# 16-wide heads' contexts turned in 32x32 blocks on VectorE, first loads on two queues, half of pass 2's masks on VectorE

## The chip, the cores and the metric

The kernel runs on one core of a Trainium2 chip. The metric is the device time of one execution in microseconds (us), the median of several runs. The engines are TensorE (PE), VectorE (DVE), ScalarE (ACT), GpSimd (POOL) and SyncE (SP, which here only issues DMAs). Each works through its own instructions in a fixed order and waits on semaphores.

## The reference, cut to what matters

Input is x of 32 batch elements, 256 rows of 256 float32, and a context of 120 rows of 256 for each. Four transformer layers are applied one after the other; all have 16 heads, in the first three of width 16, in the last of width 64.

```python
# layer 0: pre-norm; self-attention (causal), cross-attention, GELU feed-forward
x = x + attention(ln(x), ln(x), causal) @ W_aproj + b
x = x + attention(ln(x), context) @ Wcproj + b
x = x + gelu(ln(x) @ W_fc + b) @ W_mproj + b
# layer 1: post-norm; self-attention with one mask for all, cross-attention, ReLU feed-forward
x = ln(x + attention(x, x, mask_SxS) @ o_w + b)
x = ln(x + attention(x, context) @ co_w + b)
x = ln(x + relu(x @ lin1_w + b) @ lin2_w + b)
# layer 2: cross-attention with a mask for each element; layer 3: cross-attention, heads of width 64
x = ln(x + attention(x, context, mask_BxSxS2) @ wo)
x = ln(x + attention64(x, context) @ w_fc)
```

`attention` projects q, k and v, takes softmax(q k^T / 4) per head and multiplies by v.

## The kernel before

**Passes.** The kernel goes over the 32 elements three times: pass 1 (`l0`) is layer 0, pass 2 (`l1`) layer 1, pass 3 (`l2`) layers 2 and 3. x goes through device memory between them. Each pass is a list of steps per engine (`LISTS`), each step with a time in units of one element; `Step` adds the element's number and a start of the pass (`START`, `SPREAD`), and `run` sorts them. So several elements are in flight, and each engine's order is the sorted list. A step is named kind.key.number; key is `own` for self-attention (and layer 2's), `other` for the cross-attention of passes 1 and 2.

**One attention of 16-wide heads** (two per element in passes 1 and 2, one in pass 3; 160 in all). `project_q` and `project_k` are computed on PE and copied by ACT into `ot_raw` as float32 (named `other_words` in part for the cross-attention). DVE and POOL split them into three bfloat16 parts, and SP writes the parts to memory (`spill`) and loads them back stacked (`stack`). `scores_max` gets each row's maximum (PE, then DVE). Its negative is split too (`negate`), turned by PE (`negate_t`), copied by DVE to `nm_t` and moved by SP into the stack (`nm_rows`). `scores_exp` computes each head's scores minus the maximum, keys along partitions, and ACT takes the exponential into `probs`.

**Masks.** In pass 1 POOL zeroes what is not causal (L629). In pass 2 PE adds the mask to every head's scores by a matmul of `mask_less` with the identity. In pass 3 DVE takes the minimum of each pair of heads' probabilities and a mask of 0 and 2 (`mask_probs`, L1038).

**The context.** `probs_v` (PE, four steps of four heads) gives, for each head, 32 partitions by 256 queries: 16 rows of the unnormalised context, and a row with the sum of the probabilities. Two steps share a bank of 128x512 float32. Then:

- ACT copies the two banks to `ot_raw` (L672).
- `heads_q`, twice: PE turns it by 8 transposes in all, L1358, so that queries lie along partitions.
- `heads_rec` and `heads_q` on DVE: the reciprocal of the sums (L1069) and the product into `ctx_q` (L1076).
- `heads_t`: PE turns `ctx_q` back by 4 transposes (L1207), ACT copies it to `ctx_t`.
- `project_out`: PE multiplies `ctx_t` by the output weights.

**The first loads.** ACT issues all of them, 35 DMAs, before its first computation (L649 to L667): the vectors in columns and three weights that pass 1 wants first, the other weights and vectors of pass 1, the masks, and last the vectors of passes 2 and 3. PE's banks are eight; `take` waits until the last user of a bank has been read.

Lines of `L1140` are all matmuls through the helper `mm`.

## Time and profile before

| | |
|---|---|
| median of 3 runs | 4811.43 us (4810.87 to 4811.61) |
| profiled execution | 4819.19 us |
| its span, first to last instruction | 4817.4 us |
| PE busy | 4665.7 us, 97% |
| DVE busy | 3353.2 us, 70% |
| ACT busy | 2622.3 us, 54% |
| POOL busy | 1369.9 us, 28% |
| instructions | 101571 |

Busy time is the union of an engine's instructions. Matmuls overlap, so the time that one takes away from PE is the distance from its start to the next start, not its length. Pass 1 lies between 0 and about 1500 us, pass 2 up to about 3200, pass 3 after that.

### The profile page before, as it was taken

Reading aid. Unit: us, or ns where it says so; the run is one execution under the profiler, and the core shown is the slowest. Engines: PE = TensorE matmul, PEld = TensorE weight load, DVE = VectorE, ACT = ScalarE, POOL = GpSimd, SP = SyncE. Lnnn points to the kernel's source line nnn. Section 1 sums busy time; section 2 is a strip of 40 time slices with the busy share of each in tenths; the row PEclk is TensorE's granted clock in tenths of the full one; section 3 lists DMA queues with packets and bytes.
Section 4 is the critical chain, followed back from the end, with each engine's and each line's share of the span. In section 5 each row is a group of like instructions: output and inputs, shape, how many; then the busy total and the mean of one; then the engine's idle time right before and its main releaser. Section 6 shows DMA issues by size and latency. Waiting matters only on the chain. (4 is left out here: it accounts for less than half of the span.)

```text
span 4817.4 us, 101571 instructions
## 1 busy us (share of the span) xinstructions
PE 4665.7 (97%) x36479; PEld 3761.6 (78%) x36544; DVE 3353.2 (70%) x10821; ACT 2622.3 (54%) x6913; POOL 1369.9 (28%) x1813
## 2 busy tenths in 40 slices
PE   4999999999999999999999999989999999999998
PEld 3788888888887778878788787867777777777776
DVE  3677777777777766766667666656676766767674
ACT  1556656565665445454444544535565656565655
POOL 2343333333333123233332333322121212121212
PEclk8999999999999999999999999999999999999999
DMA  4444444444444344444444444432222222222211
GB/s 142 130 126 141 124 143 126 138 130 129 144 121 143 119 128 131 123 121 132 131 131 118 118 131 123 124 92 65 71 60 68 62 65 66 62 67 61 70 58 32
DMA packets 393288, 513.56 MB, mean 107 GB/s; under 512 B 109136, under 2 KB 360784, under 8 KB 371280
## 3 DMA queue, kind: packets, MB, share of 16 engines
q1 hardware_dynamic: 379008, 490.25, 34.6%
q10 hardware_dynamic: 13776, 16.81, 1.2%
q8 instruction: 290, 4.75, 0.4%
q14 instruction: 214, 1.75, 0.1%
HBM read 266.30 MB, written 236.72 MB: 104 GB/s over the span
## 5 line engine op out<-in xcount | busy, mean ns | idle before, releaser
L756 ACT ACTIVATE probs_own<-bank 128x384 f32<-128x384 f32 (+2 forms) x1280 | 607.3, 570 | 682.0 <-remote 361.2
L1140 PE MATMUL bank<-ht,w_ff 128*128 128x256 f32 x2048 | 493.3, 384 | 2.3 <-ACT ht L675 2.2
L1140 PE MATMUL bank<-w_ff,ffh 128*128 128x256 f32 x2048 | 489.3, 382 | 2.0 <-DVE ffh L1113 1.5
L574 POOL TENSOR_SCALAR veps<-meanvar 128x2 f32<-128x2 f32 x256 | 77.2, 302 | 1408.7 <-DVE meanvar L915 1408.2
L1022 DVE TENSOR_REDUCE nmf_other<-bank 128x4 f32<-128x480 f32 x512 | 311.1, 650 | 158.0 <-PE bank L1140 157.6
L1140 PEld LDWEIGHTS bank<-ht,w_ff 128*128 128x128 f32 x2048 | 372.6, 191 | 58.8 <-issue 12.8
L1140 PEld LDWEIGHTS bank<-w_ff,ffh 128*128 128x128 f32 x2048 | 374.6, 190 | 49.3 <-DVE ffh L1113 2.5
L1140 PE MATMUL bank<-qstack_own,kstack_own 99*128 99x256 bf16 (+2 forms) x2560 | 397.2, 266 | 15.4 <-DMA qstack_own<-nm_t_own 8.8
L1018 DVE CUSTOM_DVE_ANT_0 bank<-bank,mask_rows 128x256 f32<-128x256 f32 x1024 | 393.3, 463 | 13.0 <-PE bank L1140 13.0
L841 ACT ACTIVATE probs_other<-bank,negmax 128x120 f32<-128x120 f32 x1024 | 355.5, 375 | 43.9 <-DVE negmax L1120 43.9
L1140 PE MATMUL bank<-kstack_own,qstack_own 96*128 96x256 bf16 (+2 forms) x3072 | 353.7, 245 | 18.3 <-DMA qstack_own<-q_parts 16.1
L643 POOL TENSOR_TENSOR other_parts<-other_words,other_parts 128x240 bf16<-128x240 f32 (+1 forms) x128 | 114.5, 904 | 846.8 <-issue 418.1
L1140 PE MATMUL bank<-ht,w_own 128*128 128x256 f32 x1280 | 314.7, 389 | 24.1 <-ACT ht L675 24.1
L1140 PEld LDWEIGHTS bank<-qstack_own,kstack_own 99*128 99x128 bf16 (+1 forms) x2560 | 230.5, 106 | 118.2 <-DMA qstack_own<-nm_t_own 27.5
L1140 PEld LDWEIGHTS bank<-kstack_own,qstack_own 96*128 96x128 bf16 x3072 | 252.4, 98 | 89.0 <-issue 14.1
L756 ACT ACTIVATE probs_other<-bank 120x512 f32<-120x512 f32 x512 | 283.1, 611 | 57.3 <-PE bank L1140 54.2
L1140 PE MATMUL bank<-probs_own,v_aug_own 128*32 128x256 f32 (+2 forms) x5120 | 292.3, 364 | 6.9 <-POOL probs_own L629 1.6
L1018 DVE DVE_READ_ACCUMULATOR2_ANT nmf_own<- 128x1 f32 x2048 | 289.3, 141 | 0.0
L1140 PEld LDWEIGHTS bank<-ht,w_own 128*128 128x128 f32 x1280 | 232.9, 192 | 70.0 <-issue 42.9
L643 POOL TENSOR_TENSOR k_parts_own<-ot_raw_own,k_parts_own 128x512 bf16<-128x512 f32 (+1 forms) x96 | 96.0, 1000 | 652.7 <-DVE k_parts_own L975 652.7
L1120 DVE TENSOR_REDUCE negmax<-bank 128x4 f32<-128x480 f32 x256 | 155.8, 650 | 179.8 <-PE bank L1140 178.8
L1018 DVE CUSTOM_DVE_ANT_0 bank<-bank,m_rows 128x120 f32<-128x120 f32 x1024 | 247.7, 322 | 44.1 <-PE bank L1140 44.1
(172 smaller groups left out, 10899.1 us busy)
## 6 DMA issues: line engine op xcount, KB each, us to landing
qstack_own<-q_parts SPq DMA_DIRECT2D x96, 768.0 KB, 7.1
kstack_own<-k_parts SPq DMA_DIRECT2D x64, 768.0 KB, 5.5
qstack_other<-q_parts SPq DMA_DIRECT2D x64, 768.0 KB, 5.8
q_parts<-q_parts_own SPq DMA_DIRECT2D x96, 384.0 KB, 2.6
k_parts<-k_parts_own SPq DMA_DIRECT2D x64, 384.0 KB, 2.6
q_parts<-q_parts_own SPq DMA_DIRECT2D x96, 256.0 KB, 2.2
q_parts<-other_parts SPq DMA_DIRECT2D x64, 384.0 KB, 2.6
other_words<-k_parts SPq DMA_DIRECT2D x64, 360.0 KB, 3.4
```

Source lines behind the costliest of these rows:

```text
L574: nc.gpsimd.tensor_scalar(veps[key][:, :], meanvar[key][:, :, 1], r["norms"][key]["eps"], None, ALU.add).then_inc(veps_ready.sem, 1)
L643: nc.gpsimd.tensor_tensor(f3[2], x32, f3[1], ALU.subtract).then_inc(lo_ready.sem, 1)
L756: nc.scalar.activation(probs[key][0:rows, j % a.slots, 0:n], bank_of(u)[0:rows, 0:n], ACT.Exp, scale=a.scale).then_inc(a_done.sem, 1)
L841: ins = nc.scalar.activation(probs3[:, j % 4, n, :], bank[:, n * S2:(n + 1) * S2], ACT.Exp, scale=-1.0, bias=negmax3[:, j, n:n + 1], accum ...
L1018: ins = v.tensor_tensor_reduce(scores, scores, add, -1.0, LIMIT if a.masked == "each" else 3.0e38, ALU.add, ALU.min, nmf[key][:, t, at:at ...
L1022: ins = v.tensor_reduce(nmf[key][:, t, first:first + FT * len(heads) - FT + 1:FT], bank[:, 0:len(heads) * nk].rearrange("p (h k) -> p h k" ...
L1120: v.tensor_reduce(negmax3[:, j, :], bank_of(u)[:, 0:HG * S2].rearrange("p (h k) -> p h k", k=S2), AX_X, ALU.min).then_inc(negmax3_ready.se ...
L1140: return nc.tensor.matmul(out, lhsT, rhs, start=first, stop=True, skip_group_check=True)
```

## The change

**Turning the contexts.** `heads_q` and `heads_t` are gone, and with them 12 PE transposes and 3 ACT copies per attention. DVE's transpose works on blocks of 32x32, each turned in its place. DVE now reads each `probs_v` bank and writes it to `ot_raw` with all blocks turned (128x512, twice), takes the reciprocal of the 128x32 sums (`heads_rec`), multiplies (`heads_mul`, two operations of 256 elements) and turns the 128x512 `ctx_q` back in blocks into `ctx_t` (`heads_back`). The rows of the output weights are permuted on the host to fit the order in which the contexts then lie.

```diff
+            elif kind == "probs_v":
...
+                v.transpose(ot_raw[key][:, 2 * j:2 * j + 2, :].rearrange("p g x -> p (g x)"), bank_of(u, ("probs_v", key, 2 * j))[:, :]).then_inc(
+                    d_done.sem, 1)
...
             elif kind == "heads_rec":
-                if w.new(d_full, ("heads_q", key, j)):
-                    dve.wait_ge(d_full.sem, w.value(d_full, ("heads_q", key, j)))
-                by_head = bank_of(u, ("heads_q", key, j))[:, :].rearrange("p (h x) -> p h x", h=H)
-                v.reciprocal(rec[key][:, j, :], by_head[:, :, D]).then_inc(recip_ready.sem, 1)
-            elif kind == "heads_q":
-                if w.new(recip_ready, ("heads_rec", key, j)):
-                    dve.wait_ge(recip_ready.sem, w.value(recip_ready, ("heads_rec", key, j)))
-                if w.new(a_full, ("heads_t", key, 0), 1):
-                    dve.wait_ge(a_full.sem, w.value(a_full, ("heads_t", key, 0), 1))
-                by_head = bank_of(u)[:, :].rearrange("p (h x) -> p h x", h=H)
-                v.tensor_tensor(ctx_q[key][:, j, :].rearrange("p (h d) -> p h d", d=D), by_head[:, :, 0:D],
-                                rec[key][:, j, :, None].broadcast_to((P, H, D)), ALU.mult).then_inc(d_done.sem, 1)
+                for tag in w.latest_first(d_done, [("probs_v", key, i) for i in range(2)]):
+                    if w.new(d_done, tag):
+                        dve.wait_ge(d_done.sem, w.value(d_done, tag))
+                v.reciprocal(rec[key][:, :], ot_raw[key][:, :, :].rearrange("p g (b x) -> p (g b) x", x=32)[:, :, D]).then_inc(recip_ready.sem, 1)
+            elif kind == "heads_mul":
+                if w.new(recip_ready, ("heads_rec", key, 0)):
+                    dve.wait_ge(recip_ready.sem, w.value(recip_ready, ("heads_rec", key, 0)))
+
+                src = ot_raw[key][:, :, :].rearrange("p (a i) (b x) -> p a i b x", a=2, x=32)
+                dst = ctx_q[key][:, :, :].rearrange("p t c -> p (t c)").rearrange("p (a b i d) -> p a i b d", a=2, i=2, d=D)
+                by = rec[key][:, :].rearrange("p (a i b) -> p a i b", a=2, i=2)
+                for n in range(2):
+                    ins = v.tensor_tensor(dst[:, n], src[:, n, :, :, 0:D], by[:, n, :, :, None].broadcast_to((P, 2, T // 32, D)), ALU.mult)
+                ins.then_inc(divided.sem, 1)
+            elif kind == "heads_back":
+                if w.new(divided, ("heads_mul", key, 0)):
+                    dve.wait_ge(divided.sem, w.value(divided, ("heads_mul", key, 0)))
+                if w.new(d_full, ("project_out", key, 0), 1):
+                    dve.wait_ge(d_full.sem, w.value(d_full, ("project_out", key, 0), 1))
+                v.transpose(ctx_t[key][:, :, :].rearrange("p f t -> p (f t)"), ctx_q[key][:, :, :].rearrange("p t c -> p (t c)")).then_inc(
+                    context_ready.sem, 1)
```

PE's `project_out` waits for `heads_back`, and ACT's `project_q` and `project_k` of the next element wait for `heads_mul`:

```diff
-                tag = latest(w, d_full, "heads_q", key, QT, 1)
-                if w.new(d_full, tag, 1):
-                    act_e.wait_ge(d_full.sem, w.value(d_full, tag, 1))
+                if w.new(divided, ("heads_mul", key, 0), 1):
+                    act_e.wait_ge(divided.sem, w.value(divided, ("heads_mul", key, 0), 1))
...
             elif kind == "project_out":
                 arrive(key + "_o")
-                if w.new(a_done, ("heads_t", key, 0)):
-                    pe.wait_ge(a_done.sem, w.value(a_done, ("heads_t", key, 0)))
+                if w.new(context_ready, ("heads_back", key, 0)):
+                    pe.wait_ge(context_ready.sem, w.value(context_ready, ("heads_back", key, 0)))
```

**Masks.** In pass 2 the heads with an even number get `mask_probs` on DVE instead of the mask matmul; the odd ones keep it. The setup has four more operations: three with the first five, and one after a PE step `masks`, which stands at 1.25 in pass 1's first element.

```diff
-              "dve", "pe")
+              "dve", "half")
...
+            masks.l1.1/1.25
...
+            ff_mid.ff.2/3.8731 ff_out.ff.0/4.1553 masks.l1.0/1.2 masks.l1.1/1.3
```

**First loads.** ACT keeps four of them. Eighteen go to SP, right after the first load of x; the thirteen for passes 2 and 3 go to SP too, one by one at 4.00 to 7.00 elements.

```diff
+            if kind == "loads":
+
+                if key == "first":
+                    for dst, src in passes[0]["v_loads"]:
+                        sp.dma_start(dst, src).then_inc(v_loaded, 16)
+                    for n in ("other_qkv", "own_o"):
+                        for dst, src in passes[0]["weights"][n][1]:
+                            sp.dma_start(dst, src).then_inc(arrived[n], 16)
+                    for dst, src in passes[0]["late_loads"]:
+                        sp.dma_start(dst, src).then_inc(late_loaded, 16)
+                    for n in ("other_o", "ff1", "ff2"):
+                        for dst, src in passes[0]["weights"][n][1]:
+                            sp.dma_start(dst, src).then_inc(arrived[n], 16)
+                    for dst, src in mask_loads:
+                        sp.dma_start(dst, src).then_inc(masks_loaded, 16)
+                else:
+                    dst, src = rest_loads[j]
+                    sp.dma_start(dst, src).then_inc(rest_loaded, 16)
...
     @block.scalar
     def _(act_e):
         w = Where()
-        for sem, loads in (first_loaded, passes[0]["first_loads"]), (v_loaded, passes[0]["v_loads"]):
-            for dst, src in loads:
-                act_e.dma_start(dst, src).then_inc(sem, 16)
-            if sem is first_loaded:
-                for dst, src in passes[0]["weights"]["own_qkv"][1]:
-                    act_e.dma_start(dst, src).then_inc(arrived["own_qkv"], 16)
-        for n in ("other_qkv", "own_o"):
-            for dst, src in passes[0]["weights"][n][1]:
-                act_e.dma_start(dst, src).then_inc(arrived[n], 16)
-        for dst, src in passes[0]["late_loads"]:
-            act_e.dma_start(dst, src).then_inc(late_loaded, 16)
-        for n in ("other_o", "ff1", "ff2"):
-            for dst, src in passes[0]["weights"][n][1]:
-                act_e.dma_start(dst, src).then_inc(arrived[n], 16)
-        for dst, src in mask_loads:
-            act_e.dma_start(dst, src).then_inc(masks_loaded, 16)
-        for one in passes:
-            for dst, src in one["rest_loads"]:
-                act_e.dma_start(dst, src).then_inc(rest_loaded, 16)
+        for dst, src in passes[0]["first_loads"]:
+            act_e.dma_start(dst, src).then_inc(first_loaded, 16)
+        for dst, src in passes[0]["weights"]["own_qkv"][1]:
+            act_e.dma_start(dst, src).then_inc(arrived["own_qkv"], 16)
         act_e.wait_ge(first_loaded, 16 * len(passes[0]["first_loads"]))
```

**Orders.** All lists, `START` and `SPREAD` have other numbers, so every engine's order differs. The places that the prediction speaks of follow.

PE in the middle of pass 2, before. The last `probs_v` of the own attention stands first, then come weights of the next projection, the 8 turns of L1358, small transposes, and the 4 turns of `ctx_q_own` (L1207). `project_out` (`w_own,ctx_t_own`) stands six rows after the end of this piece:

```order
L1140 MATMUL bank<-probs_own,v_aug_own 32x256 x16
L1140 MATMUL bank<-ht,w_own 128x256 x4
L1358 MATMUL bank<-ident,ot_raw_own 128x128 x8
L1188 MATMUL bank<-ident,c_in 128x120 x2
L1297 MATMUL bank<-identb,nm_parts_other 96x128 x2
L1207 MATMUL bank<-ident,xh 128x128 x4
L1140 MATMUL bank<-ht,w_own 128x256 x4
L1140 MATMUL bank<-ht,w_ff 128x256 x4
L1140 MATMUL bank<-qstack_other,other_words 120x256 x10
L1207 MATMUL bank<-ident,ctx_q_own 128x128 x4
```

The same place after. The turns are gone, and `project_out` is the fifth row:

```order
L1148 MATMUL bank<-probs_own,v_aug_own 32x256 x16
L1148 MATMUL bank<-ht,w_own 128x256 x4
L1300 MATMUL bank<-identb,nm_parts_other 96x128 x2
L1148 MATMUL bank<-ht,w_own 128x256 x4
L1148 MATMUL bank<-w_own,ctx_t_own 128x256 x4
L1148 MATMUL bank<-qstack_other,other_words 120x256 x10
```

`project_out` has moved close behind the last `probs_v`.

DVE at this place of pass 2, before (names in brackets are the semaphores that it waits for):

```order
L1064 COPY nm_t_other<-bank 48x256 [waits nm_rows_other,d_full]
L1069 RECIPROCAL rec_own<-bank 128x16
L965 CAST k_parts_own<-ot_raw_own 128x512 [waits a_done,spilled_k_own]
L969 TENSOR_TENSOR ot_raw_own<-ot_raw_own,k_parts_own 128x512 [waits hi_ready]
L975 CAST k_parts_own<-ot_raw_own 128x512 [waits rest_ready,spilled_k_own]
L1069 RECIPROCAL rec_own<-bank 128x16
L1076 TENSOR_TENSOR ctx_q_own<-bank,rec_own 128x256 [waits recip_ready]
L965 CAST q_parts_own<-ot_raw_own 128x512 [waits a_done,spilled_q_own]
L1076 TENSOR_TENSOR ctx_q_own<-bank,rec_own 128x256
```

And after: masks (`mask_cols`), the two block transposes from the banks, the reciprocal, the product, and the transpose back, with steps of other attentions between them:

```order
L1024 TENSOR_TENSOR probs_own<-probs_own,mask_cols 128x512 [waits a_done] x4
L1039 TENSOR_TENSOR nmf_other<-nmf_other,nm_parts_other 128x32 [waits negate_step]
L1041 CAST nm_parts_other<-nmf_other 128x2x16 [waits negate_step]
L1062 STREAM_TRANSPOSE ot_raw_own<-bank 128x512 [waits lo_ready,a_full] x2
L1068 RECIPROCAL rec_own<-ot_raw_own 128x32 [waits d_done]
L1043 TENSOR_TENSOR nm_parts_other<-nmf_other,nm_parts_other 128x2x16 [waits negate_step]
L1077 TENSOR_TENSOR ctx_q_own<-ot_raw_own,rec_own 128x2x8x16 [waits recip_ready]
L1077 TENSOR_TENSOR ctx_q_own<-ot_raw_own,rec_own 128x2x8x16
L1050 COPY nm_t_other<-bank 48x256 [waits nm_rows_other,d_full]
L1084 STREAM_TRANSPOSE ctx_t_own<-ctx_q_own 128x512 [waits divided]
```

The whole turn is now on DVE, behind four of the eight masks.

DVE's first element after, from the negation to the first copy of `nm_t_own`; before, the five setup operations that existed stood behind that copy:

```order
L1039 TENSOR_TENSOR nmf_own<-nmf_own,nm_parts_own 128x32 [waits negate_step]
L1041 CAST nm_parts_own<-nmf_own 128x2x16 [waits negate_step]
L1043 TENSOR_TENSOR nm_parts_own<-nmf_own,nm_parts_own 128x2x16 [waits negate_step]
L1622 TENSOR_SCALAR b_root<-columns_l 128x8 [waits masks_loaded,first_loaded]
L1623 TENSOR_SCALAR mask_rows<-ffh 128x512 [waits setup_v]
L1624 TENSOR_TENSOR vectors_l<-vectors_l,ffh 128x256 [waits setup_v]
L1625 TENSOR_TENSOR vectors_l<-vectors_l,ffh 128x256 [waits setup_v]
L1628 TENSOR_SCALAR mask_less<-ffh 128x512 [waits setup_v]
L1632 TENSOR_REDUCE none_left<-mask_rows 128x2 [waits setup_v]
L1633 TENSOR_SCALAR ffh<-none_left 128x256 [waits setup_v]
L1634 TENSOR_SCALAR mask_cols<-ffh 128x512 [waits setup_v]
L1050 COPY nm_t_own<-bank 48x256 [waits setup_v,d_full]
```

Eight setup operations now stand ahead of `nm_t_own`.

## Rows read from the trace of the kernel before

**Rows 1.** Page, part 1: busy us of each engine, share of the span, instructions

```profile
PE 4665.7 (97%) x36479; PEld 3761.6 (78%) x36544; DVE 3353.2 (70%) x10821; ACT 2622.3 (54%) x6913; POOL 1369.9 (28%) x1813
```

**Rows 2.** Windows: length; busy PE, PEld, DVE, ACT, POOL; clock; DMA share, GB/s

```profile
200.00:1400.00 1200.00, 1193.36 (x9892) 999.81 (x9891) 922.75 (x2103) 724.39 (x1665) 442.28 (x748) 1.00 0.45 132
1800.00:3000.00 1200.00, 1197.39 (x9221) 964.16 (x9265) 829.25 (x3008) 576.07 (x1234) 367.76 (x400) 1.00 0.42 125
3400.00:4600.00 1200.00, 1186.99 (x9185) 934.83 (x9187) 844.14 (x3256) 734.30 (x2482) 239.46 (x250) 1.00 0.22 64
```

**Rows 3.** Once-per-element steps: timeline and tiles x_in, m_in (ns, first and last start)

```profile
64.69 0.41 SPq L475 DMA_DIRECT2D x_in<-in_x  x1
...
L475 SPq DMA_DIRECT2D x_in<-in_x x32: 393/404/449, 0.8 to 1469.5; - x32
...
L609 POOL TENSOR_TENSOR xb<-x_in,vectors_l x32: 1264/1272/1276, 1544.7 to 3137.8; 128x512 f32<-128x512 f32 x32
...
L485 SPq DMA_DIRECT2D m_in<-in_mask_BxSxS_bk x32: 389/400/1455, 3201.3 to 4706.7; - x32
```

**Rows 4.** Timeline of PE, pass 1: start us, length us, instruction, how many

```profile
1015.82 1.99 PE L1140 MATMUL bank<-ht,w_own 128*128 128x256 f32 x8
1017.65 1.04 PE L1358 MATMUL bank<-ident,ot_raw_own 128*128 128x128 f32 x8
1018.52 1.89 PE L1140 MATMUL bank<-ht,w_own 128*128 128x256 f32 x8
1020.25 0.38 PE L1140 MATMUL bank<-qstack_other,other_words 99*120 99x256 bf16 x2
1020.47 0.60 PE L1207 MATMUL bank<-ident,ctx_q_own 128*128 128x128 f32 x4
1020.91 0.38 PE L1140 MATMUL bank<-qstack_other,other_words 99*120 99x256 bf16 x2
```

**Rows 5.** Timeline of PE, pass 2, own scores with the mask

```profile
2499.93 0.38 PE L1140 MATMUL bank<-qstack_own,kstack_own 99*128 99x256 bf16 x2
2500.15 0.38 PE L1140 MATMUL bank<-mask_less,identb 128*128 128x512 bf16 x1
2500.37 0.38 PE L1140 MATMUL bank<-qstack_own,kstack_own 99*128 99x256 bf16 x2
```

**Rows 6.** Groups by line and shape of DVE: count, busy us, mean ns

```profile
L1038 DVE TENSOR_TENSOR probs_own<-probs_own,m_cols 120x512 f32<-120x512 f32 x256 | 157.3, 685 | 12.1 <-ACT probs_own L756 10.5
...
L1076 DVE TENSOR_TENSOR ctx_q_own<-bank,rec_own 128x256 f32<-128x256 f32 x192 | 73.2, 407 | 1.3
...
L1076 DVE TENSOR_TENSOR ctx_q_other<-bank,rec_other 128x256 f32<-128x256 f32 x128 | 49.2, 405 | 0.0
L1069 DVE RECIPROCAL rec_own<-bank 128x16 f32<-128x16 f32 x192 | 48.7, 254 | 132.8 <-PE bank L1358 132.8
...
L1069 DVE RECIPROCAL rec_other<-bank 128x16 f32<-128x16 f32 x128 | 28.3, 242 | 21.5 <-PE bank L1358 21.4
```

**Rows 7.** Timeline of DVE, eleven reductions of a bank back to back

```profile
1038.32 6.67 DVE L1022 TENSOR_REDUCE nmf_own<-bank 128x2 f32<-128x512 f32 x11
```

**Rows 8.** Timeline of the first 40 us, all engines

```profile
2.85 0.49 ACTq L651 DMA_DIRECT2D vectors<-in_L_xattn_b_attn  x1
...
7.17 1.09 PE L1207 MATMUL bank<-ident,xh 128*128 128x128 f32 x4 [7.17 <-DVE xh L927]
...
15.95 0.49 ACTq L664 DMA_DIRECT2D ffh<-in_mask_by_key  x1
...
29.92 1.28 ACT L675 ACT_TABLE_LOAD   x1 [29.92 <-issue]
31.21 1.02 ACT L675 ACTIVATE ht<-bank,columns_l 128x256 f32<-128x256 f32 x2
...
37.56 2.85 SPq L499 DMA_DIRECT2D k_parts<-k_parts_own  x3
```

**Rows 9.** DMA issues: KB of each, median us from issue to landing

```profile
ffh<-in_mask_by_key ACTq DMA_DIRECT2D x1, 256.0 KB, 9.3
```

More of the change, by code:

```diff
@@ L141 @@
[L141 to L144 removed]
+            turn.0.0/0.3024 project_q.own.0/0.5346 project_k.own.0/0.5738 project_v.own.0/0.6704 scores_max.own.1/0.9469
@@ new lines @@
+            scores_exp.own.3/1.3551 scores_exp.own.10/1.3644 scores_exp.own.4/1.3690 scores_exp.own.9/1.3737
+            scores_exp.own.8/1.3829 scores_exp.own.6/1.3876 scores_exp.own.7/1.3922 probs_v.own.0/1.4049
+            scores_exp.own.11/1.4253 probs_v.own.1/1.4365 scores_exp.own.12/1.4568 scores_exp.own.14/1.4615
+            scores_exp.own.13/1.4662 scores_exp.own.15/1.4754 context.c.0/1.4846 probs_v.own.2/1.4911 probs_v.own.3/1.5143
+            project_out.own.0/1.6104 project_k.other.0/1.7256 norm.1.0/1.7869 project_q.other.0/1.8368 project_v.other.0/2.1688
@@ L145 @@
+            probs_v.other.1/2.8256 project_out.other.0/3.2565 norm.2.0/3.7117 ff_in.ff.3/3.7502 ff_in.ff.2/3.8735
+            ff_in.ff.0/3.9101 ff_in.ff.1/3.9702 ff_out.ff.0/4.0208 ff_out.ff.1/4.0808 ff_out.ff.2/4.1275 ff_out.ff.3/4.1871
         """,
         "ACT": """
-            turn.0.0/0.2824 project_k.own.0/0.5466 project_q.own.0/0.5962 scores_exp.own.1/1.2539 scores_exp.own.5/1.2634
-            scores_exp.own.0/1.2729 scores_exp.own.6/1.2919 scores_exp.own.7/1.3014 scores_exp.own.2/1.3109
@@ L411, in run @@
     recip_ready = counts("recip_ready", "DVE", ("heads_rec",))
+    divided = counts("divided", "DVE", ("heads_mul",))
+    context_ready = counts("context_ready", "DVE", ("heads_back",))
     poly_ready = counts("poly_ready", "DVE", ("ff_in",))
@@ L436, in run @@
     arrived = {n: sem(f"arrived_{n}") for n in dict.fromkeys(n for one in passes for n in one["weights"])}
-    n_rest = 16 * sum(len(one["rest_loads"]) for one in passes)
+    rest_loads = [x for one in passes for x in one["rest_loads"]]
+    n_rest = 16 * len(rest_loads)
+    assert len(rest_loads) == sum(u.tag[0] == "loads" for u in plan["SP"]) - 1
     block = ctx.enter_context(nc.Block())
@@ L858, in _ @@
                 if first and j == r["first_of"]["probs_v3"]:
-                    reuse(act_e, w, u, d_full, [("heads_q", "other", i) for i in range(QT)], u.element - 1)
+                    reuse(act_e, w, u, divided, [("heads_mul", "other", 0)], u.element - 1)
                 if w.new(a_full, u.tag):
```

355 lines of the change are left out of this document (163 added, 192 removed), and 6 rows, old and new, of the table SPREAD.

## The prediction

> **What bounds the kernel now.** I read the busy shares first [rows 1]. TensorE (PE) is busy 4665.7 of 4817.4 us; VectorE (DVE) follows at 3353.2. A whole-span share averages three passes, so I cut a window from the steady part of each [rows 2]. PE is busy 1193.4, 1197.4 and 1187.0 of 1200 us, at a granted clock of 1.00, that is its 2.4 GHz level. Of PE's 151.7 idle us only 22 lie in these 3600 us; the other 129 lie in the start, the two changes of pass and the end. So inside a pass the kernel goes at PE's pace, and work taken from PE comes off the time as long as no other engine needs the whole of it. The engine to watch is DVE: 922.8, 829.3 and 844.1 of 1200 us, or 76.9%, 69.1% and 70.3%.
>
> These shares need a time per batch element. An operation that runs once per element gives it [rows 3]: (1469.5 - 64.7)/30 = 46.8 us in pass 1, (3137.8 - 1544.7)/31 = 51.4 in pass 2, (4706.7 - 3201.3)/31 = 48.6 in pass 3. DVE then works 36.0, 35.5 and 34.2 us per element.
>
> **What PE loses: the turns.** An attention's contexts cost it 8 transposes of the raw result (L1358) and 4 of the divided one (L1207). Matmuls overlap, so I don't take a row's length but the distance to the next start [rows 4]: 8 transposes from 1017.65 to 1018.52, 0.87 us; 4 from 1020.47 to 1020.91, 0.44 us. That is 1.31 us per attention. There are 2 attentions of this kind per element in passes 1 and 2 and one in pass 3, 32 x 5 = 160, so 209.6 us. Nothing hides it, for PE is the bound.
>
> **What PE loses: half of pass 2's masks.** One mask matmul per head follows two score matmuls [rows 5]; from 2500.15 to 2500.37 it is 0.22 us. The heads with an even number lose it: 8 x 32 = 256, 56.3 us. Together 265.9 us. Per element PE loses 2.62, 2.62 + 1.76 = 4.38 and 1.31 us and would need 44.2, 47.0 and 47.3.
>
> **What DVE gains.** It loses two reciprocals and two multiplications per attention: (48.7 + 28.3 + 73.2 + 49.2)/160 = 1.25 us [rows 6]. It gets one reciprocal (0.25), two multiplications (0.77 by the same rows), and three block transposes of 128x512 float32, two from PSUM and one from SBUF. No row shows such a transpose. The nearest is another operation that reads a bank of 512 float32: eleven reductions back to back take 6.67 us, 0.606 each [rows 7]. I take t = 0.61. The bounds: 0.3, if it went at twice that pace, and 2.4, if float32 were turned in four passes. Net per attention: 3t + 0.25 + 0.77 - 1.25 = 1.6 us. A mask on DVE is pass 3's `L1038` operation, 157.3/256 = 0.61 us [rows 6]; eight are 4.9 us per element of pass 2. DVE then needs 36.0 + 3.2 = 39.2 of 44.2 us in pass 1 (89%), 35.5 + 3.2 + 4.9 = 43.6 of 47.0 in pass 2 (93%), and 34.2 + 1.6 = 35.8 of 47.3 in pass 3 (76%). It fits under PE everywhere, and in pass 2 barely. ScalarE loses three copies per attention and is no bound (54%).
>
> The Trainium skill has figures for both ways of turning. "VectorE: DVE Perf Modes", section "The three transpose paths", gives 390 ns for a 128x128 bf16 transpose on TensorE and 311 ns on VectorE; the first would make the removed PE work 1920 x 0.39 = 749 us, where this trace has 0.109 us each in a run of eight [rows 4], so the row decides. Four of the second would make t 1.24 us, an estimate from that page. "Vector Engine (DVE) Microarchitecture Reference", section 3.8, says that the transpose mode sustains one element per cycle per lane, by which t would lie with [rows 7]. The two sentences disagree by a factor of two.
>
> **What the fuller DVE costs PE.** Both engines work through fixed orders, so a late DVE stalls PE even below 100%. The place is the order quoted above for pass 2. Between the last `probs_v` matmuls and `project_out` PE has two weight groups and two small transposes, 1.83 + 0.11 + 1.73 = 3.7 us (the groups from [rows 4]; the small ones an estimate). In this time DVE must do a transpose (two, if it was late), the reciprocal, two multiplications and the transpose back, with two small operations between them: 0.61 + 0.25 + 0.77 + 0.61 + some 0.4, and a wake-up of about 0.1 to 0.2 us at each of four waits; 3.3 us. The four masks just ahead of it, 2.4 us, make any lateness of DVE visible here. Before the change fourteen rows of PE's order lay between the two and two engines shared the chain. I put the new stalls at 0.8 us per element in pass 2, 0.3 in pass 1 and 0.2 in pass 3: 42 us, an estimate, bounded by 0 (cover holds) and by about 3 us per element of pass 2 and 1 of pass 1 (128 us).
>
> Queues that wait behind DVE: ScalarE's `project_q` and `project_k` copies of the next element now wait for `heads_mul`, since both write `ot_raw`. In pass 2 their results are wanted by score matmuls that stand far behind, so I cost this at nothing; without that distance it would be part of the 128.
>
> **The start.** PE has its first transposes done at 8.3 us, then waits for ScalarE, which issues DMAs until 29.92, loads a table (1.28) and writes `ht` at 31.21 [rows 8]. With 4 DMAs instead it can follow PE at about 8.3: 22.9 us earlier. Three things eat from this. The 18 loads that go to SP took ScalarE from 2.85 to 16.44, 13.6 us [rows 8]; SP, starting at 1.3, is done at about 15, and the first spill is wanted at 37.56 - 22.9 = 14.7, so nothing is lost there. But the last of these loads landed 9.3 us after its issue [rows 9], and the spills now stand behind it on the same queue: up to 4 us. And the order puts eight setup operations on DVE, about 0.6 us each, ahead of the first `nm_t` copy, where five stood off that chain: 4 us. Gain 15 us, bounds 8 and 23. The small loads now issued from SP between elements 4 and 7 have nothing behind them that is near its due time: nothing, at most 1 us.
>
> **Changes of pass and the end.** The orders are new everywhere; the 129 idle us outside the steady windows, less the start, can shrink or grow. I take 0, bounds -15 and +15.
>
> **The sum**, in the profiled execution's time: 4817.4 - 265.9 - 15 + 42 = 4578.5 us of span. The medians lie 6 us below the profiled span (4811.4 against 4817.4), so 4572 us.
>
> **Rivals.** (A) *Transposes at twice my price*, t = 1.2. Against it stand the DVE rows with 512 float32, none of which is that long in the median. (The VectorE page's 311 ns speaks for it.) DVE would need 36.0 - 0.5 + 7.2 = 42.7 of 44.2 in pass 1 and 35.5 + 4.9 - 0.5 + 7.2 = 47.1 of 47.0 in pass 2, and the chain ahead of `project_out` grows by 1.2 to 1.8 us. With 0.6, 1.6 and 0.4 us more per element: 83 us more, 4655.
> (B) *The order stalls PE*, t as I have it: the chain in pass 2 comes 1.5 us later than its cover, plus 0.5 in pass 1: 64 us more, 4636. For it: 93% and the masks ahead of the transposes; against it: PE lost only 0.2 to 1.1% to all waits in the windows.
> (C) *Everything hides*: stalls 0 and the changes of pass gain 10: 4520.
> (D) *Slower than before: DVE becomes the bound.* With float32 turned in four passes, t = 2.4, DVE needs 36.0 - 0.5 + 14.4 = 49.9 in pass 1 (3.1 over today's pitch) and 54.3 in pass 2 (2.9 over); pass 3 still gains 1.3. 32 x 4.7 - 15 = 135 us, 4946. It is slower than now from t = 2.0 on. For it: PE does float32 at a quarter of its bf16 pace; against it: no float32 row on DVE with 512 elements is that slow.
> That the change leaves the work on PE can't be: the turns are gone from PE's order.
>
> **Chances.** Forecast (4525 to 4605) 0.63, B 0.15, A 0.10, C 0.07, D 0.04, else 0.01. The likeliest is 4572. The range takes in B and the better part of C, and stops short of A's 4655: 4522 to 4650. Faster by over 0.2%, about what a measurement can tell from no change, is all but D: 0.95; within 0.2%, 0.01; slower, 0.04.
>
> **What would show it.** The transposes' distance in a run (0.6: my price; 1.2: A; over 2: D). PE's busy us: near 4665.7 - 266 = 4400. DVE's share in the windows: 89, 93, 76%. PE's waits for `ctx_t` in pass 2: below 1 us per element, else B. The first `ht` at about 8 us and the first score matmuls some 15 us earlier. The prediction is wrong in its main step if PE in the steady windows falls below 96% busy, or if the time per element doesn't fall to about 44.5, 47.8 and 47.5.

## The result, and the profile after

The changed kernel takes 4861.43 us (median of 4 runs, 4858.97 to 4870.75) against 4811.52 us for the kernel before (4 runs, 4810.87 to 4813.22). The ratio is 1.0103, with a 95% interval of 1.0089 to 1.0118: it is 1% slower. I had forecast 4572 us, 5% faster, with 0.04 for slower. The profiled execution's span is 4858.9 us.

Part 1 of the page of after, and the three steady windows (columns as in [rows 1] and [rows 2]):

```profile
PE 4509.0 (93%) x34308; PEld 3544.2 (73%) x34372; DVE 3970.5 (82%) x11401; ACT 2371.7 (49%) x6433; POOL 1430.2 (29%) x1813
```

```profile
200.00:1400.00 1200.00, 1125.19 (x9154) 914.24 (x9151) 1011.54 (x2169) 630.31 (x1494) 436.03 (x735) 1.00 0.45 131
1800.00:3000.00 1200.00, 1132.76 (x8348) 883.01 (x8387) 1052.66 (x3219) 504.80 (x1086) 416.04 (x401) 0.98 0.43 124
3400.00:4600.00 1200.00, 1147.07 (x8680) 888.16 (x8679) 960.80 (x3252) 672.34 (x2319) 231.78 (x244) 0.99 0.21 62
```

TensorE did lose work: 4665.7 us busy in [rows 1], 4509.0 now. But it no longer works without a pause. In the windows it is busy 94%, 94% and 96%, where [rows 2] has over 99% twice and 99%; all three (95.6% in pass 3) are below the 96% that I had named as the sign of a wrong main step. VectorE rose from 3353.2 to 3970.5 us, by 617 us, where my sum gives 160 x 1.6 + 256 x 0.61 = 412.

For the pace of a pass I take the starts of VectorE's sum `xn_own` in its 5th and 28th element, over 23. Timelines of VectorE, pass 2 of after:

```profile
1807.70 0.66 DVE L1109 TENSOR_TENSOR xn_own<-bank,xb 128x512 f32<-128x512 f32 x1
...
2984.45 0.69 DVE L1109 TENSOR_TENSOR xn_own<-bank,xb 128x512 f32<-128x512 f32 x1
```

That is 1176.75/23 = 51.16 us per element. By the same measure the kernel before takes 46.84, 50.49 and 47.87 us in its three passes and the changed one 47.47, 51.16 and 49.02. All three are slower. (By the starts that [rows 3] used the changed kernel takes 48.0, 51.3 and 49.2, where I had forecast about 44.5, 47.8 and 47.5.)

**The new operations cost what I had priced.** Two block transposes in a row take 1.31 us together, so the second starts about 0.6 us after the first; the means are of single ones. In a timeline's row, what stands in square brackets is how long the engine was idle before it, and what ended that. Timeline of after, and its groups of VectorE (columns as in [rows 6]):

```profile
2533.25 1.31 DVE L1062 STREAM_TRANSPOSE other_words<-bank 128x512 f32<-128x512 f32 x2 [2.21 <-PE bank L1148]
```

```profile
L1062 DVE STREAM_TRANSPOSE ot_raw_own<-bank 128x512 f32<-128x512 f32 x192 | 133.9, 709 | 78.4 <-PE bank L1148 78.0
...
L1084 DVE STREAM_TRANSPOSE ctx_t_own<-ctx_q_own 128x512 f32<-128x512 f32 x96 | 67.6, 704 | 1.2
...
L1068 DVE RECIPROCAL rec_own<-ot_raw_own 128x32 f32<-128x32 f32 x96 | 33.9, 353 | 3.1
```

**Old operations became longer.** The norm of `xn_own` (two instructions of 128x256) is the same code in both kernels. Groups of VectorE in the window 200 to 1400, first of before, then of after:

```profile
L927 DVE TENSOR_SCALAR xh<-xn_own,meanvar,rstd 128x256 f32<-128x256 f32 x50 | 18.5, 411 | 26.3 <-POOL rstd L580 26.3
```

```profile
L913 DVE TENSOR_SCALAR xh<-xn_own,meanvar,rstd 128x256 f32<-128x256 f32 x50 | 60.8, 1256 | 17.4 <-POOL rstd L602 17.4
```

Three times as long. What lies beside them shows why. Timelines of VectorE, GpSimd (POOL) and TensorE, pass 1 of after:

```profile
714.94 1.14 DVE L1043 TENSOR_TENSOR nm_parts_own<-nmf_own,nm_parts_own 128x32 bf16<-128x32 f32 x1
...
739.68 2.44 DVE L913 TENSOR_SCALAR xh<-xn_own,meanvar,rstd 128x256 f32<-128x256 f32 x2 [0.68 <-POOL rstd L602]
```

```profile
714.77 1.26 POOL L631 TENSOR_TENSOR xb<-xn_other,vectors 128x512 f32<-128x512 f32 x1 [7.51 <-DVE xn_ff L1107]
...
739.54 1.16 POOL L665 TENSOR_TENSOR q_parts_own<-ot_raw_own,q_parts_own 128x512 bf16<-128x512 f32 x1
740.65 1.32 POOL L631 TENSOR_TENSOR xb<-x_in,vectors 128x512 f32<-128x512 f32 x1
```

```profile
716.22 0.28 PE L1300 MATMUL bank<-identb,nm_parts_own 128*96 128x128 bf16 x2 [0.72 <-DVE nm_parts_own L1043]
...
742.17 0.66 PE L1210 MATMUL bank<-ident,xh 128*128 128x128 f32 x4 [1.40 <-DVE xh L913]
```

A subtraction of 32 columns, 0.19 us elsewhere, starts 0.17 us after GpSimd's sum and ends at 716.08, 0.05 us after it. The norm starts at 739.68 and ends at 742.12, when GpSimd's second operation has ended at 741.97. TensorE stands waiting for both. The masks of pass 2 are held up in the same way; timelines of VectorE, GpSimd and TensorE:

```profile
2506.93 2.75 DVE L1024 TENSOR_TENSOR probs_own<-probs_own,mask_cols 128x512 f32<-128x512 f32 x4
...
2510.89 4.65 DVE L1024 TENSOR_TENSOR probs_own<-probs_own,mask_cols 128x512 f32<-128x512 f32 x4
```

```profile
2511.06 2.26 POOL L637 TENSOR_TENSOR xb<-xh,vectors_l 128x512 f32<-128x512 f32 x1 [2.24 <-issue]
2513.40 1.59 POOL L641 TENSOR_TENSOR xb<-xb,vectors_l 128x512 f32<-128x512 f32 x1
```

```profile
2515.68 1.49 PE L1148 MATMUL bank<-probs_own,v_aug_own 128*32 128x256 f32 x16 [2.03 <-DVE probs_own L1024]
```

Four masks take 2.75 us when GpSimd has little to do and 4.65 us when it adds beside them, and TensorE then waits 2.03 us. What TensorE waited for in after's three windows, from each window's list of waits (us, times, longest; three rows of pass 1, one of pass 2, one of pass 3), is for the most part a VectorE operation that had become longer:

```profile
PE bank L1210 <- DVE xh L913: 35.4, 25, 1.8
PE bank L1300 <- DVE nm_parts_own L1043: 19.7, 24, 2.0
PE bank L1148 <- DMA qstack_own<-nm_t_own: 17.0, 25, 2.4
...
PE bank L1148 <- DVE probs_own L1024: 46.2, 24, 2.0
...
PE bank L1148 <- DVE probs_own L1024: 41.5, 50, 1.1
```

The third row is another matter: the rows of `nm_t_own`, which SyncE moves into the stack. In the kernel before this wait is 0.9 us in the same window.

I call **blocked time** what VectorE's instructions with a GpSimd instruction beside them take beyond the median of the same instructions without one, summed over the trace. It is 99 us before and 283 us after. The norm of `xn_own` has 81 of it, pass 3's masks 65, pass 2's 54, `nm_parts_own` 23, the subtraction for `k_parts_own` 20 (29, if its instructions of 240 columns are compared with their own shape alone). Of the 283 us, 212 lie beside GpSimd's sums `xb`; of the 99 us before, only 11 do.

### The profile page after: what moved, and what is told of

Same layout as the page of the kernel before. It is cut to its first block and busy times, and to the rows that moved or that the text cites. A ratio compares the mean times of both kernels' runs of the same rounds, so it can differ in the third digit from the quotient of the medians.

```text
span 4858.9 us, 97612 instructions
## 1 busy us (share of the span) xinstructions
PE 4509.0 (93%) x34308; PEld 3544.2 (73%) x34372; DVE 3970.5 (82%) x11401; ACT 2371.7 (49%) x6433; POOL 1430.2 (29%) x1813
## 3 DMA queue, kind: packets, MB, share of 16 engines
q14 instruction: 216, 1.76, 0.1%
## 5 line engine op out<-in xcount | busy, mean ns | idle before, releaser
L762 ACT ACTIVATE probs_own<-bank 128x384 f32<-128x384 f32 (+2 forms) x1280 | 597.2, 582 | 157.8 <-PE bank L1148 156.0
L637 POOL TENSOR_TENSOR xb<-xh,vectors_l 128x512 f32<-128x512 f32 x160 | 243.6, 1523 | 718.6 <-DVE xn_other L1109 404.1
L1148 PE MATMUL bank<-probs_own,v_aug_own 128*32 128x256 f32 (+2 forms) x5120 | 331.5, 374 | 108.0 <-DVE probs_own L1024 103.1
L1148 PE MATMUL bank<-qstack_own,kstack_own 99*128 99x256 bf16 (+2 forms) x2560 | 354.5, 265 | 38.6 <-DMA qstack_own<-nm_t_own 32.3
L682 ACT ACTIVATE ht<-bank,columns_l 128x256 f32<-128x256 f32 x384 | 199.0, 578 | 373.0 <-PE bank L1210 372.1
L1148 PE MATMUL bank<-ht,w_own 128*128 128x256 f32 x1280 | 333.8, 408 | 4.6 <-DMA w_own<-in_L_xattn_W_attn 2.9
L1148 PEld LDWEIGHTS bank<-probs_own,v_aug_own 128*32 128x32 f32 (+1 forms) x5120 | 133.9, 110 | 253.3 <-DVE probs_own L1024 99.8
L1004 DVE DVE_READ_ACCUMULATOR2_ANT nmf_own<- 128x1 f32 x2048 | 311.2, 152 | 0.0
L1148 PEld LDWEIGHTS bank<-ht,w_own 128*128 128x128 f32 x1280 | 250.0, 204 | 58.3 <-issue 17.7
L665 POOL TENSOR_TENSOR other_parts<-other_words,other_parts 128x512 bf16<-128x512 f32 (+1 forms) x128 | 112.2, 896 | 592.3 <-issue 301.6
```

What stands on the lines that cost most here:

```text
L637: nc.gpsimd.tensor_tensor(xb[key][:, :, :], xh[src][:, :, :], mul[:, None, :].broadcast_to((P, QT, C)), ALU.mult).then_inc(xb_half.sem, 1)
L665: nc.gpsimd.tensor_tensor(f3[2], x32, f3[1], ALU.subtract).then_inc(lo_ready.sem, 1)
L682: return nc.scalar.activation(out, in_, ACT.Identity, scale=scale, bias=bias)
L762: nc.scalar.activation(probs[key][0:rows, j % a.slots, 0:n], bank_of(u)[0:rows, 0:n], ACT.Exp, scale=a.scale).then_inc(a_done.sem, 1)
L1004: ins = v.tensor_tensor_reduce(scores, scores, add, -1.0, LIMIT if a.masked == "each" else 3.0e38, ALU.add, ALU.min, nmf[key][:, t, at:at ...
L1148: return nc.tensor.matmul(out, lhsT, rhs, start=first, stop=True, skip_group_check=True)
```

## Theories

**T1**: GpSimd's instructions hold up VectorE's, the new orders laid them beside operations for which TensorE waits, and that ate the gain. **T2**: VectorE is too full (84%, 88% and 80% of the windows) for a fixed order, whatever GpSimd does. **T3**: the masks on VectorE are what costs. T4 (the sums' own length costs whoever waits for them) and T5 (blocked time costs wherever TensorE waits for the blocked instruction, however full VectorE is) came up on the way. Results are medians; pace is per element as above.

| kernel | us | ratio to before (95%) | pace, passes 1, 2, 3 | blocked |
|---|---|---|---|---|
| before | 4811.52 | | 46.84, 50.49, 47.87 | 99 |
| changed | 4861.43 | 1.0103 (1.0089 to 1.0118) | 47.47, 51.16, 49.02 | 283 |
| GpSimd's steps moved | 4765.37 | 0.9903 (0.9888 to 0.9918) | 45.35, 51.98, 46.77 | 67 |
| GpSimd's sums small | 4652.01 | 0.9666 (0.9649 to 0.9682) | 45.75, 47.71, 46.73 | 82 |
| changed, masks on TensorE | 4830.82 | 1.0042 (1.0027 to 1.0057) | 47.61, 49.63, 49.03 | 250 |
| turns alone | 4821.96 | 1.0020 (1.0010 to 1.0031) | 44.84, 52.24, 48.28 | 121 |
| moved and mended | 4639.52 | 0.9639 (0.9626 to 0.9652) | 45.32, 47.62, 46.77 | 66 |
| mended, masks on TensorE | 4684.72 | 0.9737 (0.9722 to 0.9752) | 45.32, 49.18, 46.78 | 66 |
| before, sums small | 4802.02 | 0.9975 (0.9966 to 0.9984) | 46.80, 50.49, 47.87 | 87 |
| loads alone | 4797.64 | 0.9969 (0.9956 to 0.9981) | 46.88, 50.49, 47.88 | 97 |
| before with a collision | 4834.79 | 1.0052 (1.0037 to 1.0066) | 47.67, 50.50, 47.86 | 125 |
| mended, pass 1 of before | 4654.31 | 0.9676 (0.9660 to 0.9692) | 44.93, 47.65, 46.79 | 118 |

Each ratio is to runs of the kernel before on the same chip; their median there was 4809.75 to 4814.02 us.

## Experiments on GpSimd's place

### Its steps moved

Steps of `LISTS` (and the time of each in its pass); all else as changed:

```diff
 l0 POOL
-xb.0.0/0.7162  xb.2.0/3.1731  split_lo_q.own.0/0.6910
+xb.0.0/0.9850  xb.2.0/3.4600  split_lo_q.own.0/0.6400
 l1 POOL, SP
-xb.0.0/0.7603  xb.3.0/4.4601  store.x.0/4.5191
+xb.0.0/0.9930  xb.3.0/4.9950  store.x.0/5.0300
 l2 POOL
-xb.1.0/2.8559
+xb.1.0/2.7000
```

> The changed kernel with only GpSimd's order moved at six steps (and one store behind it): pass 1's sum xb.0 from 0.7162 to 0.9850 and xb.2 from 3.1731 to 3.4600, split_lo_q from 0.6910 to 0.6400; pass 2's xb.0 from 0.7603 to 0.9930 and xb.3 from 4.4601 to 4.9950 (its store to 5.0300); pass 3's xb.1 from 2.8559 to 2.7000. So they lie beside VectorE's maxima (which read PSUM) or in its gaps and no longer beside its norms and masks. Nothing is left out. Blocked time below is the time by which VectorE's instructions with GpSimd beside them are longer than the median of the same ones without: 99 us before the change, 283 after. Theory T1 (GpSimd's instructions on SBUF hold up VectorE's, and VectorE's lateness stalls TensorE): blocked time falls to 100 to 150, the doubled norms and masks return to 0.41 and 0.68 us, and the time falls by 60 to 120 us, to 4740 to 4800. Rival T2 (VectorE is simply too full for its fixed order): blocked time may fall, the time stays within 15 us of 4861. Rival T3 (the masks on VectorE are what costs): no more than 20 us.

Measured 4765.37 us, 96 less than the changed kernel. Blocked time is 67 us, less than the 100 to 150 that I expected, and passes 1 and 3 gain 2.1 and 2.25 us per element. In pass 3 a single step moved: 32 x 2.25 = 72 us for the 59 us of blocked time that its masks lost. Pass 2, though, is 0.8 us slower per element than in the changed kernel. Waits of SyncE's queue and timeline of TensorE, both in its pass 2:

```profile
SPq L445 <- POOL xb L631: 75.4, 23, 3.5
SPq L445 <- POOL xb L641: 36.2, 23, 3.4
```

```profile
2508.96 1.76 PE L1148 MATMUL bank<-other_words,qstack_other 96*128 96x120 bf16 x16 [3.17 <-issue]
```

The load of x waits for `xb.0` and the store for `xb.3`, which I had both made later, and behind them stand the stacked loads that TensorE needs. The profile names no releaser for most of these pauses (`issue`). But SyncE issues the load of `other_words` at 2502.30, it lands at 2508.87, and TensorE's first matmul with it starts at 2508.96; the next experiment tests this reading. A stall had been moved, not removed. T2 and T3 don't give 96 us.

### The same, with SyncE's queue mended

```diff
 l1 POOL, SP
-xb.0.0/0.9930  load_x.x.0/0.0000  store.x.0/5.0300
+xb.0.0/0.9800  load_x.x.0/0.1150  store.x.0/5.1250
```

> The experiment with GpSimd's sums moved gained 2.1 and 2.2 us per element in passes 1 and 3 but lost 0.8 in pass 2, where SyncE's load of x waited 3.3 us for xb.0 and its store 2 us for xb.3, ahead of the stacked loads of the cross-attention, and TensorE waited 3 us per element for those. Here pass 2 only is mended: xb.0 at 0.9800 (ahead of xb.2), the load of x at 0.1150 instead of 0.0000 and the store at 5.1250, both behind the stacked loads. Nothing is left out. T1: pass 2 falls from 52.0 to 47.5 to 49 us per element (it was 47.7 where the sums were small), passes 1 and 3 stay at 45.4 and 46.8: 4765 less 32 x 3 to 4.5, 4620 to 4670, below both kernels. T2 (VectorE too full in pass 2 with the masks): pass 2 back at 51 at best, 4730.

Measured 4639.52 us, 222 us below the changed kernel and 3.6% below the kernel before: the best of all. The steady windows of this kernel, then VectorE and GpSimd in its pass 3:

```profile
200.00:1400.00 1200.00, 1174.60 (x9520) 956.97 (x9519) 996.86 (x2264) 656.49 (x1561) 471.74 (x758) 1.00 0.47 138
1800.00:3000.00 1200.00, 1182.64 (x8990) 930.76 (x8980) 1055.83 (x3462) 534.98 (x1159) 408.79 (x426) 1.00 0.46 133
3400.00:4600.00 1200.00, 1184.87 (x9022) 927.22 (x9021) 944.46 (x3338) 710.11 (x2481) 263.31 (x255) 1.00 0.22 64
```

```profile
3951.96 5.12 DVE L1024 TENSOR_TENSOR probs_own<-probs_own,m_cols 120x512 f32<-120x512 f32 x8 [0.69 <-ACT probs_own L762]
```

```profile
3948.84 2.13 POOL L637 TENSOR_TENSOR xb<-xh,vectors_l 128x512 f32<-128x512 f32 x1 [19.67 <-DVE xn_ff L1109]
3951.05 1.27 POOL L641 TENSOR_TENSOR xb<-xb,vectors_l 128x512 f32<-128x512 f32 x1
```

GpSimd's two operations now stand ahead of the masks, and eight masks take 5.12 us. In the changed kernel (timelines of VectorE and of GpSimd):

```profile
4000.80 7.07 DVE L1024 TENSOR_TENSOR probs_own<-probs_own,m_cols 120x512 f32<-120x512 f32 x8 [0.69 <-ACT probs_own L762]
```

```profile
4000.89 1.74 POOL L637 TENSOR_TENSOR xb<-xh,vectors_l 128x512 f32<-128x512 f32 x1
4002.70 1.60 POOL L641 TENSOR_TENSOR xb<-xb,vectors_l 128x512 f32<-128x512 f32 x1
```

The windows also speak against T2: VectorE is busy 1055.8 of 1200 us in pass 2, as much as in the changed kernel (1052.7), and TensorE is 98.6% busy beside it, not 94.4%.

### GpSimd's sums small

```diff
-  nc.gpsimd.tensor_tensor(xb[key][:, :, :], x[:, :, :], ...
+  nc_ = C if u.element % NB == 0 else 16
+  nc.gpsimd.tensor_tensor(xb[key][:, :, 0:nc_], x[:, :, 0:nc_], ...
```

> The changed kernel, orders untouched, where GpSimd's xb operations work on 16 of 256 columns after the first element of each pass: the rest of these sums is left out, so the residual inputs are old and the output is not the reference's. GpSimd keeps every instruction and semaphore but loses about 0.95 us from each of some 350 operations. T1: blocked time of VectorE falls from 283 to below 120 us, and the time falls by 80 to 150 us, to 4710 to 4780. T2: VectorE's own work is unchanged, so the time stays within 15 us of 4861. T3: pass 2's masks are released a little sooner, 10 to 25 us, the rest nothing.

Measured 4652.01 us, 209 less, beyond what I expected. VectorE's own work and every order are untouched, so T2 and T3 fall here too. The shorter sums also let GpSimd's other steps come sooner; but the mended kernel reaches about the same (4640) with the whole sums, so it is their place that cost, not their length.

Is it the sums' own length, for whoever waits for them (T4)? The same edit in the kernel before:

> Control: the kernel before with GpSimd's xb operations on 16 of 256 columns after the first element of each pass (the rest of these sums is left out, so the output is not the reference's). The same edit took 209 us off the changed kernel. T1: in the kernel before, VectorE has room and its blocked time is 99 us, TensorE is the bound: 0 to 20 us faster than 4812. Rival T4 (GpSimd's sums cost time of their own, for whoever waits for them, whatever VectorE does): 60 us or more faster here too.

Measured 4802.02 us, 12 less, with every pace as before to 0.04 us: the 12 us lie outside the steady parts. T4 falls.

### The collision put into the kernel before

```diff
 l0 POOL (kernel before)
-xb.0.0/0.8122
+xb.0.0/0.5600
```

> The kernel before with one step of GpSimd's order moved in pass 1: xb.0 from 0.8122 to 0.5600, so that it runs beside VectorE's norm of xn_own, as it does in the changed kernel. No other edit, nothing left out. It makes the collision in a kernel where VectorE has room (77% busy in pass 1). The norm's two instructions should be blocked there, by up to 0.85 us each, some 30 to 54 us in pass 1. If blocked time costs only where VectorE is full or late (T1 with my reading of the room), the time is within 10 us of 4812; if blocked time costs wherever TensorE waits for the blocked instruction (T5), 25 to 60 us slower, all of it in pass 1.

Measured 4834.79 us, 25.0 more than the 4809.75 beside it, all in pass 1: 32 x (47.67 - 46.84) = 27 us. Timelines of VectorE, GpSimd and TensorE in this kernel:

```profile
705.17 1.60 DVE L927 TENSOR_SCALAR xh<-xn_own,meanvar,rstd 128x256 f32<-128x256 f32 x2 [1.05 <-POOL rstd L580]
```

```profile
705.03 1.27 POOL L609 TENSOR_TENSOR xb<-x_in,vectors 128x512 f32<-128x512 f32 x1
```

```profile
706.83 0.66 PE L1207 MATMUL bank<-ident,xh 128*128 128x128 f32 x4 [0.65 <-DVE xh L927]
```

The norm has 28 us of blocked time here, and 25 to 27 us come out at the end. My reading of T1, that blocked time hurts only where VectorE is full, is wrong. With VectorE at 78% (930.2 us of the window 200 to 1400) it costs nearly its whole length, because TensorE's next step waits for that instruction. T5 holds for this instruction.

The 99 us of the kernel before must lie mostly where TensorE has other work, for in its windows TensorE is idle 22 of 3600 us in all [rows 2]. The run with the small sums doesn't test this, since the sums hold up only 11 of the 99 us. So the sum of blocked time says little by itself: in pass 1 it is 69 us before and 88 after, and what changed is which instructions were held.

## Experiments on the parts

### Masks

First the changed kernel, then the mended one, each with this edit and without pass 2's `mask_probs` steps on VectorE and their preparation:

```diff
-              "dve", "half")
+              "dve", "pe")
```

> The changed kernel with all of pass 2's masks on TensorE again: 256 mask matmuls more (0.22 us apart, 56 us), VectorE without 256 operations (218 us busy, of which 54 blocked). Nothing is left out. T3 (the masks on VectorE are what costs): pass 2 goes from 51.3 us per element to about 49, 70 to 90 us in all, near 4780; TensorE's half clock in pass 2 (51 us of its steady stretch) goes too. T1: pass 2's other blocked norms and pass 1's stay, TensorE's stalls of 2 us per element are exchanged for 1.8 us of matmuls: within 25 us of 4861. T2: like T3, since VectorE falls from 88% to 78% in pass 2.

> The mended orders with all masks of pass 2 on TensorE (256 mask matmuls 0.22 us apart more; VectorE without 256 masks). Nothing is left out. If VectorE has room once GpSimd is out of its way (T1), half the masks on VectorE are worth up to 1.76 us per element, so this one is 20 to 56 us slower than the mended orders with the half. T3 (the masks cost more on VectorE than they save on TensorE): it is faster, by 10 to 60 us.

In the changed kernel half the masks on VectorE cost 31 us (4861.43 against 4830.82); with GpSimd out of the way they save 45 us (4639.52 against 4684.72). T3 had the sign right only for that order, and the 31 us are neither what I expected of T1 (within 25) nor of T3 (70 to 90). Per element 49.18 - 47.62 = 1.56 us, against the 1.76 of my sum.

### Turns alone

The orders of before, less the turning steps. VectorE's list in pass 1, for example:

```diff
-heads_rec.own.0/1.3440  heads_rec.own.1/1.3535  heads_q.own.0/1.3561  heads_q.own.1/1.3634
+probs_v.own.1/1.2946  probs_v.own.0/1.3051  heads_rec.own.0/1.3171  heads_mul.own.0/1.3221  heads_back.own.0/1.3371
```

> One part of the change alone: the contexts are turned in blocks on VectorE, in the orders and offsets of the kernel before (TensorE's and ScalarE's steps for the turns taken out, VectorE's two bank transposes put where ScalarE's copies stood, the reciprocal, product and transpose back right behind them). All first loads from ScalarE, all masks of pass 2 on TensorE. Nothing is left out. TensorE loses 210 us. T1: GpSimd stays where it was, so VectorE's blocked time stays below 140 us and the time falls to 4640 to 4700. T2 (the fuller VectorE stalls TensorE whatever the order): 4770 to 4860. My prediction's own terms for this part: 4811 - 210 + 36 = 4640.

Measured 4821.96 us, where T1's forecast was 4640 to 4700 and T2's 4770 to 4860: T1's fails in two of three passes. Pass 1 is the fastest that any run had, 44.84, but passes 2 and 3 are slower than before. Pass 2, timelines of VectorE and TensorE:

```profile
2524.46 2.31 DVE L1006 TENSOR_REDUCE nmf_other<-bank 128x4 f32<-128x480 f32 x4
2526.69 0.69 DVE L1060 STREAM_TRANSPOSE ot_raw_own<-bank 128x512 f32<-128x512 f32 x1
```

```profile
2531.12 0.28 PE L1298 MATMUL bank<-identb,nm_parts_other 128*96 128x128 bf16 x2 [2.78 <-DVE nm_parts_other L1041]
```

The two transposes (one at 2523.83), the reciprocal and the product stand between the reductions and `nm_parts_other`, for which TensorE waits 2.78 us in every element. No blocking is needed: it is the in-order queue that my rival B speaks of, at another step. In pass 3 the chain that I did name is the one, again lengthened by GpSimd:

```profile
4020.66 1.86 DVE L1075 TENSOR_TENSOR ctx_q_own<-ot_raw_own,rec_own 128x256 f32<-128x256 f32 x2
```

```profile
4023.77 1.99 PE L1146 MATMUL bank<-w_own,ctx_t_own 128*128 128x256 f32 x8 [1.60 <-DVE ctx_t_own L1082]
```

Two products take 0.76 us elsewhere and 1.86 here, and TensorE waits 1.60 us for `ctx_t_own`. GpSimd's timeline has this beside the second product:

```profile
4020.79 1.46 POOL L620 TENSOR_TENSOR xb<-xh,vectors_l 128x512 f32<-128x512 f32 x1
```

That the number falls into T2's range doesn't make T2 right. In the windows of this run VectorE is busy 1065.3 of 1200 us in pass 1, which is the fastest, and only 862.9 in pass 2, which is slower than before; the mended kernel has 1055.8 in pass 2 and is fast. It is the order that stalls TensorE, not the share. So the turns need an order made for them; I gave them none.

### Loads alone

> One part of the change alone: the first loads on two queues (four from ScalarE, the rest from SyncE as in the changed kernel), all orders of the kernel before, turns and masks as before. Nothing is left out. My prediction's term: 15 us faster, between 8 and 23: 4789 to 4804. Rival: the first load of x, now issued ahead of them, and the spills behind 18 loads give it all back: within 4 us of 4812.

Measured 4797.64 us, 16.4 less than the 4814.02 beside it; my term was 15. Timelines of ScalarE and TensorE at the start (before: table at 29.92 in [rows 8], these score matmuls at 52.37):

```profile
8.25 1.28 ACT L681 ACT_TABLE_LOAD   x1 [8.25 <-PE bank L1213]
9.55 1.02 ACT L681 ACTIVATE ht<-bank,columns_l 128x256 f32<-128x256 f32 x2
```

```profile
35.23 0.58 PE L1146 MATMUL bank<-kstack_own,qstack_own 96*128 96x256 bf16 x2 [16.71 <-DMA qstack_own<-q_parts]
```

### The mended orders with the faster pass 1

Pass 1's lists from the turns alone, with its `SPREAD`; passes 2 and 3 from the mended kernel.

> The mended orders of passes 2 and 3 (4640 us) with pass 1 in the order of the kernel before less its turning steps, as in the experiment with the turns alone, where pass 1 took 44.84 us per element against 45.32 in the mended orders. First loads on two queues, half of pass 2's masks on VectorE. Nothing is left out. Expected 10 to 25 us faster than 4640 by pass 1's own pace, if the change of pass doesn't give it back; else 4635 to 4650.

Measured 4654.31 us, 15 more, which is neither of my two ranges. Pass 1 took 0.39 us less per element (12 us), although its blocked time is 74 us against 23 in the mended kernel; but from its last `xn_own` to the first of pass 2 went 82.2 us (1464.7 to 1546.9) against 54.3 (1482.1 to 1536.4): the change of pass gave it back twice over.

## Why the prediction was wrong

**What bounds the kernel: right.** Wherever TensorE is again 98 to 99% busy the time follows it.

**The price of the added operations: right.** Transpose 0.61 forecast, about 0.6 found, so the 1.24 us that I had worked out beside it is not what the trace shows; masks 0.64 (eight in 5.12 us) against 0.61. Only the reciprocal of 32 sums was mis-sized, 0.35 us against 0.25. VectorE with the turns alone rises by 3654.4 - 3353.2 = 301 us, of which 22 are blocked time: 279/160 = 1.74 per attention against 1.6. Rivals A and D, which hung on t, were not the case. Of the unexpected 205 us of VectorE (617 less 412) the rise in blocked time makes up 184. In the mended kernel VectorE's busy time is 3756.9, 404 more than before against my 412; it comes that near because 33 us of blocked time are gone there, and without that it would be 437.

**What TensorE loses: right in kind, the turns a third too large.** In the mended kernels its busy time falls from 4665.7 to 4506.5 (turns and loads) and 4454.3 (masks too): 159 us for the turns against 209.6, and 52 for the masks against 56.3. The 1.31 us per attention, read as distances between starts [rows 4], came out as 159/160 = 1.0 us of busy time. Why it is less, no run shows.

**The stalls: the step that failed.** I put 42 us, bounded by 128, and placed them at `project_out`. The windows of after lose 74.8, 67.2 and 52.9 us, where [rows 2] lose 6.6, 2.6 and 13.0. Times the pace over 1200, that is 2.7, 2.75 and 1.65 us per element more, some 227 us over the 32 elements of each. They are mostly waits for the norm, `nm_parts_own` and the masks; for `ctx_t_own`, my place, TensorE waits 7.9 us in the whole trace of after. In the mended kernel the same reckoning (25.4, 17.4 and 15.1 us idle) gives 0.70, 0.58 and 0.07 us, 43 us in all. That this meets my 42 us is in part luck. I had put 0.3, 0.8 and 0.2 us, for a late chain ahead of `project_out`. The largest waits of the mended kernel's windows are others: the rows of `nm_t_own` in pass 1 (14.7 us) and `nm_parts_own` in pass 2 (9.9); only in pass 3 is it `ctx_t_own` (5.7). What was missing was a term for a third engine: the orders were new on GpSimd too, and I read them for TensorE and VectorE only. The bound of 128 us left it out as well, since I drew it from the length of one chain.

Two more things add to the miss of 280 us (4858.9 against 4578.5). TensorE's busy time is 109 us over the forecast 4400. The mended kernel, with the same instructions, is 54 us over it (4454.3), by the size of the turns and masks above. The other 55 us go with the granted clock, which over the span is 0.981 in the changed kernel and 0.989 in the mended one. In pass 2's window it is 0.98, and 1.00 in the kernel before and in the mended one. From 2516.3 to 2519.5 it is 0.50, the 1.2 GHz level, after TensorE had paused for 2.03 us until 2515.68. The eight matmuls that start at 2517.10 then take 3.06 us to the next start, where [rows 4] has 1.83 for eight such. Timeline of TensorE in after:

```profile
2517.10 3.22 PE L1148 MATMUL bank<-ht,w_own 128*128 128x256 f32 x8
2520.16 0.28 PE L1300 MATMUL bank<-identb,nm_parts_other 128*96 128x128 bf16 x2
```

With pauses of 3.17 us, in the run with GpSimd's steps moved, the window's clock was 0.96. In the mended kernel it is 1.00 in all three windows.

**The start: right** (15 us against 16.4). **The sum of the parts**, in orders that fit: loads 16, masks 45, and the turns what remains of 174 us, 113, against my 15, 56 and 210 less the stalls. The mended kernel's 4639.52 lies inside my range, but it is not the kernel that I predicted, and it gets there with less from the turns than I had counted on.

**What the trace of before showed already.** It has 99 us of blocked time; [rows 6] and [rows 7] are of operations that don't show it. The mean of a group hides it: the subtraction for `q_parts_own` takes 691 ns alone and 1487 with GpSimd beside it, in one row. Its mean of 960 ns, against 692 for the same shape of `k_parts_own`, was the sign to look into.

## What to carry to other kernels

Where an order is rewritten, read every engine's new neighbours, not only those of the operations that moved: here the places of six steps of GpSimd and two of SyncE, which no part of the change is about, cost it 222 us. An operation that became longer without a change of shape is the sign; look at what the other engine does from its start to its end. A blocked instruction costs nearly its whole delay if TensorE's next step waits for it (25 of 28 us here), and little where TensorE has other work, so place GpSimd's work beside reductions of banks, and check which queues (loads and stores here) then wait for it.
